# Table parts of five and three tiles, the split of the maxima a step earlier, and far rows loaded for three units at a time

## What is computed

```python
q, k, v = split_heads(x @ Wq + bq), split_heads(x @ Wk + bk), split_heads(x @ Wv + bv)   # 16 heads of 16
scale = sqrt(16 * 3)
scores = einsum('bhqd,bhkd->bhqk', q, k) / scale
pos_k = rel_embeddings @ Wk + bk                                   # 128 buckets
c2p = take_along_axis(einsum('bhqd,hpd->bhqp', q, pos_k), clip(rel + 64, 0, 127))
p2c = take_along_axis(einsum('bhkd,hpd->bhkp', k, pos_k), clip(-rel + 64, 0, 127))
scores = scores + (c2p + p2c.swapaxes(-1, -2)) / scale
ctx = softmax(scores) @ v
```

## Time and profile before

| | us |
|---|---|
| median of 3 runs (1993.77 to 2002.08) | 1996.8 |
| the profiled execution | 2003.63 |
| its span, first to last instruction | 2001.7 |
| TensorE busy | 1698.0 (85%) |
| VectorE busy | 1370.7 (68%) |
| ScalarE busy | 1121.8 (56%) |
| GpSimd busy | 1069.1 (53%) |
| SyncE's DMA queue, share of the 16 engines' time | 65.2% |

### The profile page before, as it was taken

One profiled execution on the slowest core, in us unless ns is written; L12 is line 12 of the kernel. 1 busy time (PEld: TensorE's weight loads), 2 busy tenths in 40 slices (PEclk: granted clock), 3 DMA queues, 4 the chain that ended last, 5 costly groups with the idle time before them and its releaser, 6 DMA issues. The chain is left out here.

```text
span 2001.7 us, 40568 instructions
## 1 busy us (share of the span) xinstructions
PE 1698.0 (85%) x13688; PEld 1159.6 (58%) x13688; DVE 1370.7 (68%) x3938; ACT 1121.8 (56%) x2233; POOL 1069.1 (53%) x1268
## 2 busy tenths in 40 slices
PE   1882389999999999999999999999973674999997
PEld 1451156565656566566565666566532464999996
DVE  1673188788888788898798899899843553343343
ACT  1672257676767677677677777677751460222221
POOL 0210267676777667667576777777711451233332
PEclk6996589999999999999999999999996675999998
DMA  4598778777777777777877777787718852676772
GB/s 113 188 303 274 225 250 262 246 237 251 245 261 248 256 247 240 257 254 245 265 237 251 249 261 250 240 272 246 235 44 215 284 176 86 198 212 215 223 219 78
DMA packets 320826, 453.36 MB, mean 226 GB/s; under 512 B 35132, under 2 KB 260303, under 8 KB 320526
## 3 DMA queue, kind: packets, MB, share of 16 engines
q1 hardware_dynamic: 308034, 415.25, 65.2%
q10 hardware_dynamic: 7596, 21.10, 3.4%
q0 software_dynamic: 4992, 14.43, 1.9%
HBM read 257.32 MB, written 193.65 MB: 225 GB/s over the span
## 5 line engine op out<-in xcount | busy, mean ns | idle before, releaser
L865 ACT ACTIVATE t_probsT<-t_flip 128x512 f32<-128x512 f32 x1024 | 619.2, 607 | 242.7 <-PE t_flip L756 117.5
L814 DVE TENSOR_REDUCE t_most<-t_scores 128x1 f32<-128x640 f32 (+1 forms) x512 | 436.7, 853 | 169.8 <-PE t_scores L740 166.5
L833 DVE TENSOR_SCALAR t_band<-t_band,t_top 128x384 f32<-128x384 f32 (+1 forms) x512 | 383.8, 750 | 0.0
L859 ACT COPY t_table<-t_table_ps 128x512 f32<-128x512 f32 x512 | 298.2, 582 | 70.7 <-issue 41.1
L777 PE MATMUL t_sum_ps<-t_probsT,t_vals 128*32 128x256 f32 x4096 | 329.5, 394 | 0.2 <-ACT t_probsT L865 0.2
L926 POOL TENSOR_TENSOR t_near<-t_near,t_masks 128x384 f32<-128x384 f32 (+1 forms) x128 | 146.8, 1147 | 338.9 <-DMA t_near<-skew_d 336.4
L942 POOL TENSOR_TENSOR t_near<-t_near,t_masks 128x768 f32<-128x768 f32 (+1 forms) x128 | 272.4, 2129 | 0.0
L763 PE MATMUL t_flip<-t_masks,t_band 128*128 128x128 f32 x1408 | 263.0, 276 | 0.0
L818 DVE CUSTOM_DVE_ANT_0 t_band<-t_scores,t_near 128x384 f32<-128x384 f32 (+1 forms) x512 | 262.1, 512 | 0.0
L740 PE MATMUL t_scores<-t_masks,t_near 128*128 128x128 f32 x1408 | 243.5, 277 | 7.1 <-POOLq L945 7.1
L733 PE MATMUL t_scores<-t_after,t_quest 105*128 105x256 bf16 (+3 forms) x1024 | 244.9, 289 | 2.6 <-DVE t_most L818 2.4
(11 more groups left out here) (186 smaller groups left out, 2343.7 us busy)
## 6 DMA issues: line engine op xcount, KB each, us to landing
skew_d<-t_table SPq DMA_DIRECT2D x128, 1024.0 KB, 8.9
t_near<-skew_d SPq DMA_DIRECT2D x128, 640.0 KB, 6.2
t_near<-skew_d SPq DMA_DIRECT2D x128, 384.0 KB, 4.8
e_w<-in_L_ffn_W_dram ACTq DMA_DIRECT2D x39, 512.0 KB
e_w<-in_L_ffn_W_dram SPq DMA_DIRECT2D x39, 512.0 KB
split_d<-p_part SPq DMA_DIRECT2D x32, 384.0 KB
t_after<-split_d SPq DMA_DIRECT2D x64, 192.0 KB
t_quest<-split_d SPq DMA_DIRECT2D x64, 192.0 KB
```

Of the source, the lines that this page charges most:

```text
L814: nc.vector.tensor_reduce(most[:, c, 1:2], out[:, wide:S], AX.X, ALU.max)
L833: nc.vector.tensor_scalar(band[n % 2][:, t, 0:wide], band[n % 2][:, t, 0:wide], top[n % 2][:, t:t + 1], None, ALU.subtract).then_inc(level ...
L859: nc.scalar.copy(table[n % 2][:, h, :, u % 4, :], table_ps[:, :, :]).then_inc(table_kept, 1)
L865: nc.scalar.activation(probsT[s % 3][:, half * 512:(half + 1) * 512], flip_ps[half][:, :], ACT.Exp, scale=SCALE).then_inc(expd, 1)
```

## The change

- The table parts that are written hold tiles 0 to 4 and 5 to 7 (`TILES`) instead of 0 to 3 and 4 to 7. The pieces that are read, and of which the edges are made, are tiles 0 to 3 and 4 to 7. So the first write waits for a fifth table copy, score tile 3 needs the first piece, and the edge steps run over four and three tiles instead of three and four.
- GpSimd's order: the split of the maxima stands after steps 0 and 1 of the second piece. Step 2 comes behind it.
- The far rows are loaded for three units by each transfer (`load_far`, every third unit, two units ahead of the first of them). They have a semaphore of their own, `far_in`, for which the first score of a unit waits. `make_table` and `twin` wait for the two big transfers alone. The six buffers of a stack become one tensor.

```diff
-    HATS = 5
+    HATS = 2
+    FARS = 3
-    PIECES = ((0, 3), (3, QT))
-    EDGES = ((0, 3), (3, QT - 1))
+    TILES = ((0, 5), (5, QT))
+    PIECES = ((0, 4), (4, QT))
+    EDGES = ((0, 4), (4, QT - 1))
...
-        quest, after, before = ([sb(f"{w}{i}", [ROWS, S], BF16) for i in range(BUFS)] for w in ("quest", "after", "before"))
+        quests, afters, befores = (sb(w, [ROWS, BUFS, S], BF16) for w in ("quests", "afters", "befores"))
+        quest, after, before = ([t[:, i, :] for i in range(BUFS)] for t in (quests, afters, befores))
...
-                for dst, far_at, many in ((quest[i][FAR:FAR + 6, :], n * (2 * far), 2 * PARTS),
-                                          (after[i][KROWS:FAR, :], (N + n) * (2 * far) + far, PARTS),
-                                          (before[i][KROWS:FAR, :], (N + n) * (2 * far), PARTS)):
-                    sp.dma_start(dst, view(far_d, far_at, [[S, many], [1, S]])).then_inc(hats_in[i], 16)
+
+            def load_far(n):
+                i, many = n % BUFS, min(FARS, N - n)
+                if n >= BUFS:
+                    sp.wait_ge(flipped, 2 * QT * (n + many - BUFS))
+                for dst, far_at, rows_many in ((quests[FAR:FAR + 6, i:i + many, :], n * (2 * far), 2 * PARTS),
+                                               (afters[KROWS:FAR, i:i + many, :], (N + n) * (2 * far) + far, PARTS),
+                                               (befores[KROWS:FAR, i:i + many, :], (N + n) * (2 * far), PARTS)):
+                    sp.dma_start(dst, view(far_d, far_at, [[S, rows_many], [2 * far, many], [1, S]])
+                                 ).then_inc(far_in[i // FARS], 16)
...
             def skew_write(n, h):
-                sp.wait_ge(table_kept, n * QT + 4 * h + 4)
+                lo, hi = TILES[h]
+                sp.wait_ge(table_kept, n * QT + hi)
...
             def skew_read(n, h):
                 if n >= 2:
-                    sp.wait_ge(scored, (n - 2) * QT + 4 * h + 4)
-                    sp.wait_ge(seen, (n - 2) * QT + 4 * h + 4)
+                    sp.wait_ge(scored, (n - 2) * QT + TILES[h][1])
+                    sp.wait_ge(seen, (n - 2) * QT + TILES[h][1])
...
                 if 0 <= u + 4 < N:
                     load_unit(u + 4)
+                if 0 <= u + 2 < N and (u + 2) % FARS == 0:
+                    load_far(u + 2)
...
                 if t == 0:
                     pe.wait_ge(twin_made, n + 1)
+                    pe.wait_ge(far_in[i // FARS], 16 * 3 * (n // BUFS + 1))
...
-                pe.wait_ge(near_made, n * 2 + (1 if t < 3 else 2))
+                pe.wait_ge(near_made, n * 2 + (1 if t < 4 else 2))
...
-            steps = ((2, 0, (0, 1)), (3, 0, (2,)), (4, 0, (3,)), (5, 0, (4,)),
-                     (6, 1, (0, 1)), (7, 1, (2,)), (8, 1, (3,)), (9, 1, (4,)))
+            steps = ((3, 0, (0, 1)), (4, 0, (2,)), (5, 0, (3,)), (6, 0, (4,)), (7, 1, (0, 1)), (8, 1, (2, 3)), (9, 1, (4,)))
...
-                if t == 4 and 0 <= u + 2 < N:
+                if t == 5 and 0 <= u + 2 < N:
                     keep_side(u + 2, 0)
```

More of the change, by code:

```diff
@@ L583, in attend @@
         ones, after_rows, before_rows = (sb(w, [9, S], BF16) for w in ("ones", "after_rows", "before_rows"))
-        quest, after, before = ([sb(f"{w}{i}", [ROWS, S], BF16) for i in range(BUFS)] for w in ("quest", "after", "before"))
+        quests, afters, befores = (sb(w, [ROWS, BUFS, S], BF16) for w in ("quests", "afters", "befores"))
+        quest, after, before = ([t[:, i, :] for i in range(BUFS)] for t in (quests, afters, befores))
         rows = sb("rows", [KROWS, H, 2, 2 * P], BF16)
         vals = [sb(f"vals{i}", [P, QT, VROW]) for i in range(2)]
-        table = [sb(f"table{i}", [P, 2, 2, 4, SPOT]) for i in range(2)]
+        table = [sb(f"table{i}", [P, 2, QT, SPOT]) for i in range(2)]
         side = [sb(f"side{i}", [P, 2, QT]) for i in range(2)]
@@ L606, in attend @@
         hats_in = [sem(f"t_hats_in{i}") for i in range(BUFS)]
+        far_in = [sem(f"t_far_in{i}") for i in range(BUFS // FARS)]
         top_in = [sem(f"t_top_in{i}") for i in range(BUFS)]
@@ L654, in skew_write @@
                     sp.wait_ge(skew_in[n % 2][1], 16 * 2 * (n // 2))
-                sp.dma_start(view(skew_d, n % 2 * (P * PITCH) + h * 4 * SPOT + 1, [[PITCH, P], [TABLE, 2], [1, 4 * SPOT]]),
-                             table[n % 2][:, h, :, :, :].rearrange("p a u v -> p a (u v)")).then_inc(skew_out[n % 2][h], 16)
+                sp.dma_start(view(skew_d, n % 2 * (P * PITCH) + lo * SPOT + 1, [[PITCH, P], [TABLE, 2], [1, (hi - lo) * SPOT]]),
+                             table[n % 2][:, :, lo:hi, :].rearrange("p a u v -> p a (u v)")).then_inc(skew_out[n % 2][h], 16)
             def skew_read(n, h):
                 if n >= 2:
-                    sp.wait_ge(scored, (n - 2) * QT + 4 * h + 4)
-                    sp.wait_ge(seen, (n - 2) * QT + 4 * h + 4)
+                    sp.wait_ge(scored, (n - 2) * QT + TILES[h][1])
+                    sp.wait_ge(seen, (n - 2) * QT + TILES[h][1])
                 sp.wait_ge(skew_out[n % 2][h], 16 * (n // 2 + 1))
@@ L814, in look @@
                 nc.vector.tensor_reduce(most[:, c, 1:2], out[:, wide:S], AX.X, ALU.max)
-                dve.wait_ge(near_made, n * 2 + (1 if t < 3 else 2))
+                dve.wait_ge(near_made, n * 2 + (1 if t < 4 else 2))
                 if n >= 2:
@@ L853, in keep_table @@
                 n, u = x // QT, x % QT
-                h = u // 4
+                h = 0 if u < TILES[0][1] else 1
                 act.wait_ge(table_made, x + 1)
-                if u % 4 == 0 and n >= 2:
+                if u == TILES[h][0] and n >= 2:
                     act.wait_ge(skew_out[n % 2][h], 16 * (n // 2))
                     act.wait_ge(side_kept, (n - 2) * 2 + h + 1)
-                nc.scalar.copy(table[n % 2][:, h, :, u % 4, :], table_ps[:, :, :]).then_inc(table_kept, 1)
+                nc.scalar.copy(table[n % 2][:, :, u, :], table_ps[:, :, :]).then_inc(table_kept, 1)
             def exponent(s, half):
@@ L910, in keep_side @@
             def keep_side(n, h):
-                pool.wait_ge(table_kept, n * QT + 4 * h + 4)
+                lo, hi = TILES[h]
+                pool.wait_ge(table_kept, n * QT + hi)
                 if n >= 2:
-                    pool.wait_ge(edge_made, (n - 2) * 10 + (5 if h == 0 else 10))
-                nc.gpsimd.tensor_copy(side[n % 2][:, :, 4 * h:4 * h + 4], table[n % 2][:, h, :, :, BAND]).then_inc(side_kept, 1)
+                    pool.wait_ge(edge_made, (n - 2) * 10 + 10)
+                nc.gpsimd.tensor_copy(side[n % 2][:, :, lo:hi], table[n % 2][:, :, lo:hi, BAND]).then_inc(side_kept, 1)
             def edge(n, h, step):
```

## The result

The changed kernel takes 2077.4 us (median of 4 runs) against 1998.8 us of the kernel before, a ratio of 1.040 with a 95% interval of 1.037 to 1.043. It is slower; the forecast was 1994 us with a range up to 2016. The profiled execution took 2081.12 us, 77.5 us more than the one before.

A forecast was written before the change was run, and what follows sets the result against it. SyncE's loop of write, landing and read was taken as the bound. Read and write mix +3 us, far rows -5, start and end with the early split -0.7: about -3 from 1996.8, so 1994 us, range 1972 to 2016.

The forecast's parts named there:

- What bounds the kernel: SyncE's loop of write, landing and read in the attention stage sets the pace, 19.23 us a unit on average.
- Rival (2): TensorE's wait at the transpose was the bound after all: its 50.6 us go, 1946 us; chance 0.08.
- The early split: GpSimd's split of the maxima: transpose 2.6 us earlier against the read, paid out once at the stage's end.
- The fifth table: SyncE's first write waits for a fifth table copy, in time by 1.29 us; costed at nothing.
- The other piece: The first piece, grown to four tiles, could come about 0.2 us late for TensorE, taking back some of 2.6 us once.
- The far rows: Small loads joined for three units: 0.08 us a round less, -5 us in all.
- by bytes: Lower end of the far rows' gain: no fewer bytes are loaded, so nothing is gained; by number it was 14 us.
- The bytes of A and B: Moving a read tile into A and a written tile into B costs +0.05 us a round, +3 us in 63 rounds.
- A: Stretch from first to second read in SyncE's loop, 8.20 us; forecast 8.48 to 8.54; its tail follows the read's landing.
- B: Stretch from second read to the next first read in SyncE's loop, 10.74 us; forecast 10.46 to 10.53.
- A + B over 19.2 us: Sign in SyncE's read intervals: a round this long would mean that the read mix is at fault.
- Rival (3): The read loop gets longer: A takes +0.34 us a round, B gives nothing back, +21 us, 2018 us; chance 0.17.

The follow-up runs named there:

- e6_split: The kernel before with nothing but the split of the maxima after two steps of the second piece instead of three: 2007.1 us, ratio 1.002.
- the two controls: The changed kernel, row pitch unchanged, with the skewed tables' DRAM tensor made larger, or also its second buffer moved 128 KB: 2082 and 2078 us.
- e3_writes: The kernel before with table parts written as five and three tiles; pieces read, GpSimd's order and far rows as before: 2003.6 us, ratio 1.001.
- e1_tables: The changed kernel without its far rows' part, far rows loaded for each unit as before: 2070.4 us, ratio 1.034 against the kernel before.

## Why the prediction was wrong

**What bounds the kernel: right.** The loop of write, landing and read is the metronome. Its round times 63 gives the time of all these kernels but for a few us, TensorE waits more where the round is longer (from 0.5 us of each round of 18.44 to 2.0 of 20.44), and taking 1.0 us of GpSimd's work away ahead of the split (e6_split) gave nothing. Rival (2), that TensorE's wait is the bound, has fallen.

**The early split: right, and alone of no worth that shows (1.002).** In this round GpSimd starts the second piece's steps at 899.53, the split at 901.46, and the first piece's steps at 910.41; the transpose runs at 902.84:

```profile
899.53 1.19 POOL L941 TENSOR_TENSOR t_near<-t_near,t_masks 128x384 f32<-128x384 f32 x1 [1.62 <-DMA t_near<-skew_d]
...
901.46 0.25 POOL L967 CAST t_top_part<-t_top 128x8 bf16<-128x8 f32 x1
...
910.41 1.28 POOL L941 TENSOR_TENSOR t_near<-t_near,t_masks 128x512 f32<-128x512 f32 x1 [3.91 <-DMA t_near<-skew_d]
```

```profile
902.84 0.23 PE L799 MATMUL t_table_ps<-t_ident,t_top_part 128*24 128x128 bf16 x1 [1.24 <-POOL t_top_part L977]
```

The transpose stands 10.19 us behind the read's issue (892.65), against 12.21 before and 9.60 forecast; the two steps take 1.93 instead of 1.74 us, and the read lands 0.4 us later than I had it. That this is a phase, paid once, fits e6_split; no run shows the 2.6 us apart.

**The fifth table: right**, it is hardly waited for (22.0 us in 28 waits of the whole stage, 11.3 in 11 before). **The other piece: right in kind**, L754 now waits 14.4 us in 14 units, little beside the 88.3 at the transpose.

**The far rows: the term was -5 us and measured nothing** (1.0014, interval 0.9996 to 1.0031). The end "by bytes" was the true one. The rule to join small transfers, which the prediction takes from the Trainium skill (DMA: Bandwidth & Descriptors, "Rules for kernel authors"), paid nothing here; look first whether the transfers stand in the loop. In the changed kernel the join may cost something: it lies at 1.040, without the join at 1.034; but the two controls, which have it, lie at 1.036 and 1.035, so it isn't told apart.

**The bytes of A and B: the step that failed.** It has two mis-sized terms. I took a four-tile read at the middle of three and five, 6.48 us, and let A's write tail shrink with its bytes from 2.74 to about 2.0 us. Measured in the round shown, the read takes 910.41 - 903.64 = 6.77 us in A and 899.53 - 892.65 = 6.88 in B, and A's tail is 9.47 - 6.77 = 2.70 us, hardly shorter at all. A: forecast 8.48 to 8.54, measured 9.47. B: 6.88 + 4.11 = 10.99, forecast 10.46 to 10.53. Over all units the four pieces came to +1.24 and -0.14 us (A's read and tail), -0.51 and +0.62 (B's), 1.21 together; forecast were +1.02, -0.7, -1.02 and +0.7 to 0.8. So the two reads missed by 0.7 us a round and A's tail by nearly 0.6. The prediction's own sign for this, A + B over 19.2 us, came: 20.46 in the round shown.

That it is the pieces, and not the writes by themselves, e3_writes and e1_tables show: the writes alone leave the round as it was (A -0.44, B +0.50 us in the medians), and with the pieces of four on top A grows by 1.67 and B gives back 0.53. The trace of before held only reads of three and five tiles, and a line through two sizes can't show a bend. Why A's tail doesn't shrink behind a four-tile read stays open; that it does so with the gap (2.31 us) ties it to the distance of the rows.

**Rival (3) had the place and the condition right** (A longer, B gives nothing back) and its price too small: +0.34 us a round, because it too used the straight line and the shorter tail, where 1.20 came. So the range's upper end fell short by 60 us. A bound from both sides should have taken the four-tile read at the five-tile one's 7.50 us, which nothing in the trace excluded, and left A's tail at 2.74: 10.24 us in place of 8.20, and the range would have held the result.

## What to carry to other kernels

Where a queue waits for its own transfers, as here, the round of these can be the time, and the engines' waits behind it only its shadow: look at the intervals between repeated issues before costing any wait. When transfers are cut in other sizes, don't draw a line through the two sizes that the trace has; the new size may cost as much as the larger one, so price it there as the worse end, and don't let the transfer behind it shrink with its bytes before a run has shown it. A gap between rows that lie a round 16 KB apart is a short trial: here it was worth 1.2%, and with the loads spread over all transfer engines 2.7%.

## What the hardware did that I had not expected

- The same writes and reads take longer when their rows in DRAM lie exactly 16 KB apart: B is 10.70 us with 16 KB, 9.84 with 17 KB (before), and 10.84 against 9.91, 9.79 and 9.99 with 16.25, 17 and 32 KB (after).
- The time of a read is bent over its size: two transfers of 384, 512 and 640 KB (three, four and five tiles of both tables), issued together, have both landed after 5.6, 6.8 to 6.9 and 7.4 us. With the gap and the loads spread the bend is nearly gone: 5.5, 6.5 and 7.2.
- Two loads that use the transfer engines at a share of 0.43 cost the loop almost nothing while rows have no gap, and 0.76 us of A once they have one.
